# A four-layer graph network with norms on one core: the order of the second graph layer's DVE work, its output bias, and the addition ahead of the first norm

## The chip, the cores and the metric

One core of a Trainium2 chip runs the whole program. The metric is the device time of one execution in microseconds (us). Lower is better.

## The reference

There are 100,000 nodes with 16 features each, 50,000 edges sorted by destination, 16 features on each edge, and one of 8 types for each. Four layers follow one another, each added to its input and normed over the 16 features of a node:

```python
x = _layernorm(x + _L0_gnn_ref(x, edge_attr_16, ..., src, dst))   # per edge and feature a softmax over the edges of a node
x = _layernorm(x + _L1_gnn_ref(x, edge_index, W_tp, weight, bias))  # bilinear messages
x = _layernorm(x + _L2_gnn_ref(x, edge_index, eps1, w1a, ..., b2b)) # two graph layers, then log_softmax
x = _layernorm(x + _L3_gnn_ref(x, src, dst, edge_type_8, ...))      # typed messages, then a GRU cell

def _gin_conv(x, src, dst, eps, wa, ba, wb, bb, n_nodes):           # used twice in _L2
    agg = jax.ops.segment_sum(x[src], dst, num_segments=n_nodes)
    h = (1.0 + eps) * x + agg
    return jax.nn.relu(h @ wa + ba) @ wb + bb
def _layernorm(x, axis=-1, eps=1e-05):
    m = jnp.mean(x, axis=axis, keepdims=True)
    v = jnp.var(x, axis=axis, keepdims=True)
    return (x - m) / jnp.sqrt(v + eps)
```

The change touches the first norm, `x + _L0(x)`, and the second `_gin_conv` with its log_softmax and the third norm.

## The kernel before, in words

**Tiles.** Nodes are padded to 14 tiles (NODE_TILES) of 7168. A tile is 128 partitions x 896 columns (W): 56 nodes of 16 features on each partition, in 7 packs of 128 columns. Five engines run programs of their own (PE, DVE, ACT, POOL and SP, which issues the plain DMAs), each strictly in the order written; semaphores tie them together, and the order in the code is the schedule. The stages follow one another on the same node tables: the edge softmax; the first norm with the start of the sum by source; the bilinear layer; a sum by destination; `gin(0)`, the first graph layer; another sum by destination; `gin(1)`, the second graph layer; a third sum by destination; the GRU.

**First norm** (DVE from L1883, ACT from L972, PE from L1310, SP from L641). For each tile DVE adds the two loaded tiles `xin` and `ain` (L1884), sums over 16 features (L1751), centres into `xm` (L1753), sums the squares that ACT made (L1763; ACT's Square is L922), and scales with the factor that ACT made (L928 and L930) into the resident table `x1s` (L1770). From tile 3 on most tiles also carry one group of the expansion, which takes finished rows to slots of edges: ACT copies 8 blocks (L948), PE multiplies them with one-hot tiles (L1318), DVE makes the one-hot tile (L1783), masks the products (L1793) and reduces them (L1805), and POOL adds them into a table (L738). That is so for 10 of the 14 tiles; the other four (0 to 2 and 10) have the norm alone. PE's program holds only the expansion products there, and SP loads tile t+2 once tile t is scaled. After the last tile come further groups, and then POOL scatters 56 groups with 392 indirect DMAs (L755).

**Second graph layer**, `gin(1)`. In every tile DVE makes `yy` (L2033, `gin_ahead`), PE turns it (L1433), ACT copies that (L1089), PE multiplies with the first weights (L1444, L1445), ACT adds the bias and takes the Relu (L1098), and PE multiplies with the second weights, pack by pack, into `ps[2]` (L1456, `gin_out`). Then DVE adds the output bias into `zz` (L2040), takes the maximum over a node's 16 values (L2067) and subtracts it into `zcs` (L2072). ACT takes Exp (L1112), DVE sums (L2080), ACT takes Ln (L1120). POOL adds the layer's input to `zcs` (L794) and subtracts the logarithm (L797), in `gin_second`. Then the norm: DVE sums (L2088), centres into `xm` (L2091), ACT squares (L1127), DVE sums the squares (L2098), ACT makes the factor (L1134, L1136), and DVE scales (L2105). One round of DVE's loop (from L2109) reads:

```python
gin_ahead(1, t + 3)
gin_scale(t - 1)
gin_softmax(t + 1)      # L2040, L2067, L2072
if t < NODE_TILES:
    gin_centre(t)       # L2088, L2091
gin_sum(t + 1)
if t < NODE_TILES:
    gin_squares(t)
```

PE's round is `gin_out(t - 2)`, `gin_hidden(t - 1)`, `gin_turn(t)`; PE may write `ps[2]` again once L2040 has read it (semaphore `g_o`). SP (from L547) waits, tile by tile, for `yy` and then loads `xin`, for POOL's addition and then loads `ain`, for the scaling and then stores `yout`. After the last store POOL starts the gathers of the third sum by destination (L771).

## Time and profile before

| | |
|---|---|
| device time, 3 runs | 4698.01 us median, 4685.06 to 4700.72 |
| the profiled execution's own time | 4688.55 us |
| its span | 4686.7 us |
| granted TensorE clock, mean | 0.703 |
| DVE busy | 3340.9 us (71%) |
| POOL busy | 3240.6 us (69%) |
| PE busy | 2956.8 us (63%) |
| ACT busy | 1618.6 us (35%) |
| the chain that ended last | POOL 14%, issue 9%, DVE 5%, PE 3% |

Times are those of one execution, taken by the hardware profiler. Times of a timeline count from the start of the span. A line number is that of the instruction in the kernel; L440 and other helpers serve several callers. A group's mean covers the time of one instruction; the time from the start of one to the start of the next can be shorter, as consecutive ones overlap a little. The granted clock is the share of TensorE's full clock that the throttle passed in a stretch: 1.00 is 2.4 GHz and 0.50 is 1.2 GHz.

### The profile page before, as it was taken

To read this page: it belongs to the slowest core of one execution; us is meant where nothing else is said; L and a number is where in the kernel's file an instruction comes from. 1 tells how busy PE (TensorE), PEld (TensorE's weight loads), DVE (VectorE), ACT (ScalarE), POOL (GpSimd) and SP (SyncE) were. 2 spreads that over 40 slices of the span, in tenths; PEclk is the share of its full clock that TensorE was granted. 3 is DMA by queue.
4 is the path that set the end of the run, shared out by engine and by line. 5 is a ranking of instruction groups with operands and counts; after the bars stand their busy time and mean duration, and the time that the engine had idled before them with its cause. 6 is when DMAs were issued, how large, how long until landed. Compare 5 with 4: busy or idle time off the path is not lost. (4 is left out here: it accounts for less than half of the span.)

```text
span 4686.7 us, 58419 instructions
## 1 busy us (share of the span) xinstructions
PE 2956.8 (63%) x13925; PEld 2319.0 (49%) x13925; DVE 3340.9 (71%) x5631; ACT 1618.6 (35%) x4208; POOL 3240.6 (69%) x2831
## 2 busy tenths in 40 slices
PE   5888888888534444435999344473444546777686
PEld 2444444444334444434888234453344436777675
DVE  7999999999795555555888455663556784555678
ACT  3666666666441111102555111121111241222245
POOL 4777777777537888887999677726777337777422
PEclk8777778777665555557999566576556665555688
DMA  4222222222143333343322100031000240000022
GB/s 128 69 67 63 69 69 65 69 63 66 42 135 58 60 60 59 57 76 81 79 78 63 18 7 7 7 93 33 7 7 7 53 114 7 7 7 7 3 74 76
DMA packets 411137, 247.46 MB, mean 53 GB/s; under 512 B 107063, under 2 KB 370091, under 8 KB 410988
## 3 DMA queue, kind: packets, MB, share of 16 engines
q1 hardware_dynamic: 291708, 226.22, 17.4%
q0 software_dynamic: 119296, 19.68, 6.5%
q8 instruction: 58, 0.95, 0.1%
q14 instruction: 75, 0.61, 0.0%
HBM read 180.94 MB, written 64.76 MB: 52 GB/s over the span
## 5 line engine op out<-in xcount | busy, mean ns | idle before, releaser
L1375 PE MATMUL ps<-arena 128*128 128x128 f32 x2976 | 665.7, 413 | 619.3 <-DVE arena L1934 564.6
L771 POOL DMA_INDIRECT extra<-x_t,srci x784 | 767.1, 978 | 260.5 <-issue 245.3
L1375 PEld LDWEIGHTS ps<-arena 128*128 128x128 f32 x2976 | 618.3, 316 | 656.5 <-issue 647.6
L755 POOL DMA_INDIRECT sums<-cmb,sidx x392 | 613.1, 1564 | 136.3 <-issue 117.8
L1248 PE MATMUL ps<-arena,yout 128*128 128x512 f32 x784 | 565.3, 812 | 219.6 <-DVE arena L1725 210.3
L717 POOL DMA_INDIRECT xg<-in_x,xidx x392 | 443.8, 1132 | 203.6 <-issue 118.8
L704 POOL DMA_INDIRECT ft_t<-fts,fidx x392 | 469.2, 1197 | 146.6 <-issue 115.8
L1934 DVE TENSOR_TENSOR arena<-jmask,ps 128x1024 f32<-128x1024 f32 (+1 forms) x174 | 212.5, 1221 | 499.5 <-ACT ps L1030 491.4
L1951 DVE TENSOR_TENSOR arena<-arena,ps 128x128 f32 x1488 | 426.3, 286 | 182.0 <-DVE arena L1951 23.9
L771 POOL DMA_INDIRECT extra<-h_t,srci x392 | 369.9, 944 | 215.5 <-issue 210.9
L1318 PE MATMUL ps<-arena 128*128 128x128 f32 x992 | 224.6, 417 | 445.1 <-DVE arena L1783 347.0
L1030 ACT ACTIVATE ps<-extra 128x16 f32 x1392 | 160.2, 168 | 944.5 <-SPq L666 819.0
L1318 PEld LDWEIGHTS ps<-arena 128*128 128x128 f32 x992 | 208.1, 319 | 453.2 <-DVE arena L1783 352.7
L1417 PE MATMUL ps<-wb,arena 128*128 128x256 f32 x1568 | 355.3, 380 | 0.0
L1248 PEld LDWEIGHTS ps<-arena,yout 128*128 128x128 f32 x784 | 191.5, 259 | 311.7 <-DVE arena L1725 227.9
L1417 PEld LDWEIGHTS ps<-wb,arena 128*128 128x128 f32 x1568 | 291.2, 191 | 35.7
L440 POOL TENSOR_TENSOR extra<-arena 128x512 f32<-128x512 f32 x196 | 267.5, 1386 | 32.3 <-DVE arena L2005 16.1
L1681 DVE TENSOR_TENSOR_SCAN arena<-ps,arena,edge_in 128x512 f32<-128x512 f32 x196 | 240.5, 1268 | 10.3 <-PE ps L1250 10.3
L1699 DVE TENSOR_TENSOR_SCAN arena<-arena,ps 128x512 f32<-128x512 f32 x196 | 240.2, 1268 | 10.2
L1925 DVE TENSOR_TENSOR arena<-ps,relp 128x1024 f32<-128x1024 f32 x186 | 226.3, 1217 | 8.2 <-PE ps L1375 8.2
L1705 DVE TENSOR_TENSOR_SCAN arena<-arena 128x1026 f32<-128x1026 f32 x98 | 222.5, 2270 | 0.0
L960 ACT ACTIVATE cmb<-ps 128x112 f32<-128x112 f32 x56 | 14.7, 263 | 587.8 <-PE ps L1333 360.1
(257 smaller groups left out, 6407.5 us busy)
## 6 DMA issues: line engine op xcount, KB each, us to landing
edge_in<-in_ef SPq DMA_DIRECT2D x98, 256.0 KB
edge_in<-far_row SPq DMA_DIRECT2D x98, 256.0 KB
ain<-in_src_row SPq DMA_DIRECT2D x56, 448.0 KB, 3.7
sums<-zero SPq DMA_DIRECT2D x132, 144.0 KB
arena<-rel_t SPq DMA_DIRECT2D x63, 256.0 KB, 3.9
x_t<-yout SPq DMA_DIRECT2D x28, 448.0 KB, 3.4
xin<-x_t SPq DMA_DIRECT2D x28, 448.0 KB, 4.0
extra<-x_t,srci POOLq DMA_INDIRECT x784, 2.3
```

Source lines behind the costliest of these rows:

```text
L440: return eng.tensor_tensor(o.rearrange("p (s w u) -> p s w u", s=2, u=F), products.rearrange("p (s w u) -> p s w u", s=2, u=F), x_tile.rea ...
L704: pool.indirect_dma_start(ft_t, bass.IndirectOffsetOnAxis(ap=fidx[b][:, k:k + 1], axis=0), fts[b][:, k * F:(k + 1) * F], None).then_inc(ft ...
L717: pool.indirect_dma_start(xg[:, k, :], None, x, bass.IndirectOffsetOnAxis(ap=xidx[:, k:k + 1], axis=0)).then_inc(x_gathered, 16)
L755: pool.indirect_dma_start(sums[k], bass.IndirectOffsetOnAxis(ap=sidx[n % 2][:, j:j + 1], axis=0), cmb[n % 2][:, j, :], None, compute_op=AL ...
L771: pool.indirect_dma_start(dy[:, t, :], None, table, bass.IndirectOffsetOnAxis(ap=srci[:, t:t + 1], axis=0)).then_inc(d_gathered[n % QUEUE] ...
L1248: pe.matmul(o, wl[:, cols], outer[b][:, h * ET:(h + 1) * ET], start=True, stop=False)
L1318: last = pe.matmul(ps[b][:, j * P:(j + 1) * P], turned_oneh[b][:, j * P:(j + 1) * P], xblk[b][:, j * P:(j + 1) * P], start=True, stop=True)
L1375: last = pe.matmul(slot_sums(k, n)[:, j * P:(j + 1) * P], oneh[b][:, j * P:(j + 1) * P], placed[b][:, j * P:(j + 1) * P], start=True, stop ...
L1417: last = pe.matmul(bank_of(k)[:, 256 * s:256 * (s + 1)], sT[par_], wbk[j // 4][:, (j % 4) * 256:(j % 4 + 1) * 256], start=True, stop=True)
L1681: last = dve.tensor_tensor_scan(mx[b][:, h, 1:ET + 1], ps[0][:, h * ET:(h + 1) * ET], far[b][:, :], mx[b][:, h, 0:1], ALU.max, ALU.add)
L1699: last = dve.tensor_tensor_scan(by_half(num[o])[:, h, 1:ET + 1], by_half(dd[o])[:, h, 1:ET + 1], ps[1][:, h * ET:(h + 1) * ET], final(num[ ...
L1951: dve.tensor_tensor(o, o, slot_sums(k, c)[:, j * P:(j + 1) * P], ALU.add).then_inc(acc_done, 1)
```

## The change

In the first norm PE makes the sum of the two tiles, as two products with the identity that accumulate in `ps[3]`, for columns 0 to 511 and 512 to 895; DVE reads that sum from PSUM. DVE's round becomes: sum of tile t, scaling of tile t-1, centring of tile t, expansion, squares of tile t. ACT copies the blocks ahead of the square instead of behind it, PE puts each expansion group behind the tile's addition, and SP loads tile t+2 once PE has added tile t.

In the second graph layer PE adds the output bias: ahead of each of the 7 products of `gin_out` it multiplies a 3-row tile of ones with a 3-row tile that holds the bias as three 16-bit parts, into the same columns. L2040 is gone; the maximum and the subtraction read `ps[2]`, and PE waits for the subtraction (`l_zc`) before it writes there again. DVE's round becomes: subtraction of tile t, norm's sum of t-1, sum of exponentials of t, squares of t-2, maximum of t+1, scaling of t-2, centring of t-1, `yy` of t+4. ACT's round is put in a matching order. SP waits for POOL's addition before it loads `ain` two tiles on, and stores five tiles behind in place of two. `split_bias`, 10 small DVE instructions, runs once behind the sum by source. New tiles and the semaphore `bias_split` serve that.

```diff
@@ -255,2 +255,4 @@
         vvs = [vv[:, :], tile_of(13)]
+        out_bias, out_ones = sb("out_bias", [PARTS, P], BF16), sb("out_ones", [PARTS, P], BF16)
+        out_part, out_rest = sb("out_part", [PARTS, PARTS, F], BF16), sb("out_rest", [PARTS, 4, F])
         gate_set = [extra[:, 0:4 * UNIT], arena[:, (N_ACC + 1) * UNIT:(N_ACC + 5) * UNIT]]
@@ -546,3 +550,4 @@
                 sum_by_destination(ph - 2)
-                for t in range(NODE_TILES + 2):
+                ahead = 5 if ph in late_loads else 2
+                for t in range(NODE_TILES + ahead):
                     if t + 2 < NODE_TILES:
@@ -550,8 +555,8 @@
                         load(t + 2)
-                    n = t - 2
+                    if ph in late_loads and 2 <= t < NODE_TILES:
+                        wait(l_t, t - 1)
+                        load_late(t)
+                    n = t - ahead
                     if n < 0:
                         continue
-                    if ph in late_loads and n + 2 < NODE_TILES:
-                        wait(l_t, n + 1)
-                        load_late(n + 2)
                     wait(y_done, node_count(ph, 0, n) + 1)
@@ -646,3 +651,3 @@
                 for t in range(NODE_TILES):
-                    wait(y_done, t + 1)
+                    wait(v_done, t + 1)
                     load_nodes(t + 2)
@@ -962,6 +967,2 @@
 
-                def blocks_of(t, n, at):
-                    act.wait_ge(y_done, t)
-                    copy_blocks(0, n, at)
-
                 act.wait_ge(y_zero, 2)
@@ -969,9 +970,8 @@
                 for t in range(NODE_TILES):
-                    ready = first_tile_with(0, t)
-                    if ready:
-                        at = block_offsets(0, ready[0])
-                        norm(0, t // 2, t % 2, lambda t=t, n=ready[0], at=at: blocks_of(t, n, at))
-                        copied = ready[0] + 1
-                    else:
-                        norm(0, t // 2, t % 2)
+                    for n in first_tile_with(0, t):
+                        at = block_offsets(0, n)
+                        act.wait_ge(y_done, t)
+                        copy_blocks(0, n, at)
+                        copied = n + 1
+                    norm(0, t // 2, t % 2)
                 act.wait_ge(y_done, NODE_TILES)
@@ -1132,3 +1132,3 @@
                 n = node_count(2, 0, t)
-                act.wait_ge(s_own, 2 * n + 2)
+                act.wait_ge(s_own, 2 * n + (3 if t < NODE_TILES - 1 else 2))
                 act.activation(st[:, 2, :], st[:, 1, :], ACT.Ln, bias=eps_col[:, :], scale=1.0 / F).then_inc(s_ln, 1)
@@ -1137,9 +1137,10 @@
 
-            for t in range(-3, NODE_TILES):
+            for t in range(-2, NODE_TILES + 2):
+                gin_turned(1, t + 2)
+                gin_exp(t)
+                gin_ln(t)
+                gin_factor(t - 2)
                 gin_hidden(1, t + 2)
-                gin_turned(1, t + 3)
-                gin_exp(t + 1)
-                gin_square(t)
-                gin_ln(t + 1)
-                gin_factor(t)
+                if t <= NODE_TILES:
+                    gin_square(t - 1)
             sum_by_destination(2)
@@ -1321,3 +1322,15 @@
 
-                for n in range(AHEAD + 1):
+                expanded = 0
+                for t in range(NODE_TILES):
+                    wait_loaded(pe, 0, t // 2, t % 2)
+                    if t:
+                        pe.wait_ge(s_xm, t)
+                    for cols in (slice(0, 512), slice(512, W)):
+                        pe.matmul(ps[3][:, cols], ident, xin[t % 2][:, cols], start=True, stop=False)
+                        last = pe.matmul(ps[3][:, cols], ident, ain[t % 2][:, cols], start=False, stop=True)
+                    last.then_inc(v_done, 1)
+                    for n in first_tile_with(1, t):
+                        expand(n)
+                        expanded = n + 1
+                for n in range(expanded, AHEAD + 1):
                     expand(n)
@@ -1453,6 +1466,8 @@
                 if t:
-                    pe.wait_ge(g_o, n)
+                    pe.wait_ge(l_zc if q else g_o, t)
                 for g in range(PACKS):
-                    last = pe.matmul(ps[2][:, g * P:(g + 1) * P], hidden[:, g * P:(g + 1) * P], bd[2 * q + 1][:, :],
-                                     start=True, stop=True)
+                    o = ps[2][:, g * P:(g + 1) * P]
+                    if q:
+                        pe.matmul(o, out_ones[:, :], out_bias[:, :], start=True, stop=False)
+                    last = pe.matmul(o, hidden[:, g * P:(g + 1) * P], bd[2 * q + 1][:, :], start=not q, stop=True)
                 last.then_inc(g_ops, 1)
@@ -1467,2 +1482,3 @@
             sum_by_destination(1)
+            pe.wait_ge(bias_split, BIAS_MADE)
             gin(1)
@@ -1881,12 +1897,23 @@
                 expanded = 0
-                for t in range(NODE_TILES):
-                    wait_loaded(dve, 0, t // 2, t % 2)
-                    dve.tensor_tensor(vv[:, :], xin[t % 2][:, :], ain[t % 2][:, :], ALU.add).then_inc(v_done, 1)
-                    ready = first_tile_with(1, t)
-                    if ready:
-                        norm(0, 0, t // 2, t % 2, vv[:, :],
-                             [lambda n=ready[0]: expand_mask(0, n), lambda n=ready[0]: expand_sum(0, n)])
-                        expanded = ready[0] + 1
-                    else:
-                        norm(0, 0, t // 2, t % 2, vv[:, :])
+                v = slots(ps[3][:, 0:W])
+                for t in range(NODE_TILES + 1):
+                    if t < NODE_TILES:
+                        dve.wait_ge(v_done, t + 1)
+                        dve.tensor_reduce(st[:, 0, :], v, AX, ALU.add).then_inc(s_own, 1)
+                    if t:
+                        dve.wait_ge(s_sd, t)
+                        dve.tensor_tensor(slots(x1_of(0, t - 1)), slots(xm[:, :]), over(st[:, 3, :]),
+                                          ALU.mult).then_inc(y_done, 1)
+                    if t < NODE_TILES:
+                        dve.wait_ge(s_own, 2 * t + 1)
+                        if t:
+                            dve.wait_ge(y_done, t)
+                        dve.scalar_tensor_tensor(slots(xm[:, :]), over(st[:, 0, :]), -1.0 / F, v,
+                                                 ALU.mult, ALU.add).then_inc(s_xm, 1)
+                        for n in first_tile_with(1, t):
+                            expand_mask(0, n)
+                            expand_sum(0, n)
+                            expanded = n + 1
+                        dve.wait_ge(s_sq, t + 1)
+                        dve.tensor_reduce(st[:, 1, :], slots(sq_first), AX, ALU.add).then_inc(s_own, 1)
                 keys(0, 0)
@@ -1896,2 +1923,27 @@
 
+            def split_bias():
+
+                b = prm[0:PARTS, A_B2B:A_B2B + F]
+                part = lambda k: out_part[:, k, :]
+                rest = lambda k: out_rest[:, k, :]
+                at = lambda k: ident[0:PARTS, k:k + 1]
+                dve.memset(out_ones[:, :], 1.0).then_inc(bias_split, 1)
+                dve.tensor_copy(part(0), b).then_inc(bias_split, 1)
+                dve.wait_ge(bias_split, 2)
+                dve.tensor_tensor(rest(0), b, part(0), ALU.subtract).then_inc(bias_split, 1)
+                dve.wait_ge(bias_split, 3)
+                dve.tensor_copy(part(1), rest(0)).then_inc(bias_split, 1)
+                dve.wait_ge(bias_split, 4)
...
+                dve.wait_ge(bias_split, 9)
+                dve.tensor_copy(out_bias[:, :].rearrange("p (j f) -> p j f", f=F),
+                                rest(2).unsqueeze(1).broadcast_to((PARTS, PACK, F))).then_inc(bias_split, 1)
+
             def sum_by_destination(k):
@@ -1980,2 +2032,3 @@
             sum_by_source()
+            split_bias()
 
@@ -2059,3 +2112,5 @@
 
-            def gin_softmax(t):
+            FIRST_OWN = 2 * node_count(2, 0, 0)
+
+            def gin_maximum(t):
 
@@ -2065,4 +2120,8 @@
                     dve.wait_ge(l_zc, t)
-                gin_out(1, t)
-                dve.tensor_reduce(st[:, 6, :], slots(zz), AX, ALU.max).then_inc(l_max, 1)
+                dve.wait_ge(g_ops, NODE_TILES + t + 1)
+                dve.tensor_reduce(st[:, 6, :], slots(ps[2][:, 0:W]), AX, ALU.max).then_inc(l_max, 1)
+
+            def gin_shift(t):
+                if not 0 <= t < NODE_TILES:
+                    return
                 dve.wait_ge(l_max, t + 1)
@@ -2071,3 +2130,4 @@
                     dve.wait_ge(l_ex, t - 1)
-                dve.tensor_tensor(slots(zcs[t % 2]), slots(zz), over(st[:, 6, :]), ALU.subtract).then_inc(l_zc, 1)
+                dve.tensor_tensor(slots(zcs[t % 2]), slots(ps[2][:, 0:W]), over(st[:, 6, :]),
+                                  ALU.subtract).then_inc(l_zc, 1)
 
@@ -2081,12 +2141,16 @@
 
+            def gin_total(t):
+                if not 0 <= t < NODE_TILES:
+                    return
+                dve.wait_ge(v_done, node_count(2, 0, t) + 1 - NODE_TILES)
+                if t:
+                    dve.wait_ge(s_xm, node_count(2, 0, t))
+                dve.tensor_reduce(st[:, 0, :], slots(vvs[t % 2]), AX, ALU.add).then_inc(s_own, 1)
+
             def gin_centre(t):
-                if t < 0:
+                if not 0 <= t < NODE_TILES:
                     return
-                n = node_count(2, 0, t)
-                v = slots(vvs[t % 2])
-                dve.wait_ge(v_done, n + 1 - NODE_TILES)
-                dve.tensor_reduce(st[:, 0, :], v, AX, ALU.add).then_inc(s_own, 1)
-                dve.wait_ge(s_own, 2 * n + 1)
+                dve.wait_ge(s_own, FIRST_OWN + max(2 * t, 1))
                 dve.wait_ge(y_done, node_count(3, 0, t))
-                dve.scalar_tensor_tensor(slots(xm[:, :]), over(st[:, 0, :]), -1.0 / F, v,
+                dve.scalar_tensor_tensor(slots(xm[:, :]), over(st[:, 0, :]), -1.0 / F, slots(vvs[t % 2]),
                                          ALU.mult, ALU.add).then_inc(s_xm, 1)
@@ -2108,11 +2172,11 @@
             wait_sums(dve, 1)
-            for t in range(-3, NODE_TILES + 1):
-                gin_ahead(1, t + 3)
-                gin_scale(t - 1)
-                gin_softmax(t + 1)
-                if t < NODE_TILES:
-                    gin_centre(t)
-                gin_sum(t + 1)
-                if t < NODE_TILES:
-                    gin_squares(t)
+            for t in range(-4, NODE_TILES + 2):
+                gin_shift(t)
+                gin_total(t - 1)
+                gin_sum(t)
+                gin_squares(t - 2)
+                gin_maximum(t + 1)
+                gin_scale(t - 2)
+                gin_centre(t - 1)
+                gin_ahead(1, t + 4)
             sum_by_destination(2)
```

## Rows read from the trace of the kernel before

**Rows 1.** The page's line of busy time per engine over the span
```profile
PE 2956.8 (63%) x13925; PEld 2319.0 (49%) x13925; DVE 3340.9 (71%) x5631; ACT 1618.6 (35%) x4208; POOL 3240.6 (69%) x2831
```

**Rows 2.** Windows: stretch, its us, then busy us (instructions) per engine, PEclk, DMA
```profile
1282.00:1394.00 112.00, 39.01 (x170) 36.70 (x171) 103.06 (x103) 41.50 (x130) 37.10 (x74) 0.59 0.45 127
...
3700.00:3714.00 14.00, 7.62 (x43) 5.23 (x43) 12.86 (x11) 7.57 (x12) 8.09 (x4) 0.97 0.13 38
...
3714.00:3820.00 106.00, 64.36 (x234) 48.03 (x235) 104.85 (x85) 41.74 (x65) 34.17 (x18) 0.69 0.45 119
```

**Rows 3.** Timeline, DVE, one tile of the second layer: start us, us, instruction
```profile
3772.63 1.08 DVE L2040 TENSOR_TENSOR arena<-ps,prm 128x896 f32<-128x896 f32 x1
3773.74 1.09 DVE L2067 TENSOR_REDUCE st<-arena 128x56 f32<-128x896 f32 x1
3774.86 1.09 DVE L2072 TENSOR_TENSOR extra<-arena,st 128x896 f32<-128x896 f32 x1
3775.87 1.08 DVE L2088 TENSOR_REDUCE st<-vv 128x56 f32<-128x896 f32 x1
3776.98 2.08 DVE L2091 SCALAR_TENSOR_TENSOR xm<-st,vv 128x896 f32<-128x896 f32 x1
3778.99 1.07 DVE L2080 TENSOR_REDUCE st<-extra 128x56 f32<-128x896 f32 x1
3780.08 1.09 DVE L2098 TENSOR_REDUCE st<-arena 128x56 f32<-128x896 f32 x1
3781.09 2.06 DVE L2033 SCALAR_TENSOR_TENSOR arena<-xin,prm,arena 128x896 f32<-128x896 f32 x1
3783.07 1.08 DVE L2105 TENSOR_TENSOR yout<-xm,st 128x896 f32<-128x896 f32 x1
```

**Rows 4.** Timeline, POOL, the same tile: start us, us, instruction, idle before
```profile
3776.03 2.08 POOL L794 TENSOR_TENSOR extra<-extra,ain 128x896 f32<-128x896 f32 x1 [5.28 <-DVE extra L2072]
...
3780.49 1.71 POOL L797 TENSOR_TENSOR extra<-extra,st 128x896 f32<-128x896 f32 x1 [2.37 <-ACT st L1120]
```

**Rows 5.** One line of the bilinear stage: ns min/median/max of DVE from PSUM
```profile
L440 DVE TENSOR_TENSOR arena<-ps,arena x98: 675/691/693, 2174.0 to 2573.8; 128x512 f32<-128x512 f32 x98
```

**Rows 6.** Timeline, DVE: first subtraction and last scaling of the second layer
```profile
3699.80 1.09 DVE L2072 TENSOR_TENSOR extra<-arena,st 128x896 f32<-128x896 f32 x1
...
3854.68 1.09 DVE L2105 TENSOR_TENSOR yout<-xm,st 128x896 f32<-128x896 f32 x1 [0.69 <-ACT st L1136]
```

**Rows 7.** Timeline, PE: the layer's products at either clock
```profile
3690.88 2.07 PE L1444 MATMUL ps<-arena,bd 128*128 128x512 f32 x2 [1.01 <-ACT arena L1089]
...
3705.20 1.80 PE L1456 MATMUL ps<-bd,arena 128*128 128x128 f32 x14
...
3706.84 1.02 PE L1444 MATMUL ps<-extra,bd 128*128 128x512 f32 x2
...
3773.85 3.33 PE L1456 MATMUL ps<-bd,arena 128*128 128x128 f32 x14 [0.34 <-DVE arena L2040]
```

**Rows 8.** Groups by line and shape: 16-bit matmuls of 128 columns
```profile
L1292 PE MATMUL ps<-identb,xq 128*48 128x128 bf16 x784 | 40.5, 225 | 1.4 <-ACT ain L905 1.4
```

**Rows 9.** The page's DMA issues: KB each, us to landing
```profile
xin<-x_t SPq DMA_DIRECT2D x28, 448.0 KB, 4.0
```

**Rows 10.** Timeline, DVE, first norm: first addition, one tile, last scaling
```profile
1282.11 1.08 DVE L1884 TENSOR_TENSOR vv<-xin,ain 128x896 f32<-128x896 f32 x1
...
1312.26 1.10 DVE L1884 TENSOR_TENSOR vv<-xin,ain 128x896 f32<-128x896 f32 x1
...
1320.44 1.11 DVE L1884 TENSOR_TENSOR vv<-xin,ain 128x896 f32<-128x896 f32 x1
...
1392.58 1.08 DVE L1770 TENSOR_TENSOR arena<-xm,st 128x896 f32<-128x896 f32 x1
```

**Rows 11.** Timeline, PE, first norm: one group of expansion products
```profile
1318.63 3.76 PE L1318 MATMUL ps<-arena 128*128 128x128 f32 x16 [4.64 <-issue]
```

**Rows 12.** Timeline, DVE: the wait behind the sum by source
```profile
2174.04 0.69 DVE L440 TENSOR_TENSOR arena<-ps,arena 128x512 f32<-128x512 f32 x1 [30.61 <-PE ps L1417]
```

10 lines of the change are left out of this document (added).

## The prediction

> **What bounds the kernel now.** First the page's busy shares [rows 1]: no engine is busy beyond 71%, so the kernel is a chain of stages, each with a bound of its own, and the two stages of the change have to be read by themselves. Then the windows [rows 2]: in the first norm DVE is busy for 103.06 of 112 us, in the body of the second graph layer for 104.85 of 106 us. DVE sets the pace in both, while PE has room (39 and 64 us busy) and runs at a mean granted clock of 0.59 and 0.69. Both stages stand between stages that need their whole result, so what they lose in time the kernel loses.
>
> Then DVE's timeline of one tile of the layer [rows 3]. Nine instructions make a round. The steps from start to start are 1.00 us, or 1.11 where an instruction needs the result just made, except that L2091 and L2033 take 2.08 and 2.06 us. Beside them [rows 4]: POOL's L794 runs from 3776.03 to 3778.11, and L2091, started at 3776.98, ends at 3779.06; POOL's L797 runs from 3780.49 to 3782.20, and L2033 ends at 3783.15. Both end 0.95 us behind POOL, as if begun then: a DVE instruction with two operands in SBUF stands still while POOL works. The sums L2088, L2080 and L2098 overlap POOL and take 1.07 to 1.09. The nine steps add up to 11.44 us a tile (to 3784.07, a step of 1.00 behind the last row), 2 us of it blocked.
>
> **Layer, DVE's part.** L2040 goes: 1.0 us a tile. The new order puts two sums, the sum of squares and the maximum behind the subtraction, the time in which POOL works, and scaling, centring and yy behind those. Does the subtraction or the maximum cost more for reading PSUM? L2040 reads PSUM in 1.08 us, L2072 reads SBUF in 1.09 [rows 3], and 98 DVE instructions that take one operand from PSUM and one from SBUF beside a POOL stage take 675 to 693 ns, none blocked [rows 5]. I take 1.09 for both. The Trainium skill (VectorE: DVE Perf Modes, section Rules for kernel authors) advises copying a matmul's result to SBUF where several operations follow; by it dropping L2040 gains nothing, and the sum would be 14 us smaller. The trace shows no such price for one read; two reads in a row no run here shows.
>
> The round, from the subtraction's start at 0: norm's sum at 1.0; sum of exponentials at 2.2 (it needs ACT's Exp over 896 columns, an estimate of one DVE instruction's length behind the subtraction); squares at 3.2; maximum at 4.2; scaling at 5.2. POOL's second instruction starts 1.5 us behind the start of L2080 [rows 3, 4], so at 3.7, and ends at 5.4; the scaling then ends at 6.35. Centring starts at 6.45, yy at 7.45, the next subtraction at 8.6. **8.6 us** a tile is what DVE allows.
>
> **Layer, PE's part, and the new wait.** The maximum of tile t+1 waits for PE's product, and that for the subtraction of tile t, since both use ps[2]. Behind the waiting maximum on DVE stand scaling, centring, yy and the next subtraction, and POOL waits for that. The chain is 1.15 (subtraction and signal) + product + 4.2 (maximum, scaling, centring, yy, signals) us. The product took 1.80 us at the high clock and 3.33 at the low one [rows 7]. The bias adds seven 16-bit products of 3 rows by 128 columns with a weight load each. The trace has none such. Below: 0.05 us each, as L1292 at 40.5 us for 784 [rows 8]. Above: each costs as much as the 32-bit product beside it, 1.8 us a tile more at the high clock, 3.3 at the low. I take 0.07 and 0.14 each, near L1292, to which they are nearest in type and width: 2.3 us at the high clock, 4.3 at the low. The chain gives 7.65 us (DVE's 8.6 stands) or **9.65 us**.
>
> Which clock? Before, PE stood idle for 41.6 of 106 us, 4.5 in each round, and began the burst of 3773.85 at the low clock; from 3700 to 3714 the granted clock was 0.97 [rows 2, 7]. After, the round is shorter and PE's work longer: high-clock work is 2.3 + 1.7 (L1444 of 1.02 and L1445 of three quarters of that, less overlap) + 1.0 (turning, half of L1456) = 5.0 of 8.6 us, so idle time shrinks to 3.6 us but doesn't go; at the low clock it is about 9.5 of 9.65. The two states feed on each other, and I expect a mixture: **9.2 us**.
>
> The sum: the first subtraction moves from 3699.80 [rows 6] to about 3701.0, since yy of tile 3 and the bias come before it. Two first rounds without norm work (6.2, 7.2), eight full ones (73.6), three without yy (24.6), then 7.5, 5.1 and 3.9 for the tail: 128.1 us, to 3829 in place of 3855.8 (3854.68 + 1.09, rows 6). **26 us** gained; at 8.6 a round 34, at 9.65 19.
>
> What hides the rest: SP moves the same 42 transfers. A load of xin is issued behind POOL's addition of two rounds before its use, some 12 us ahead, and lands in 4.0 [rows 9]; without that cover a round would grow by up to 4 us. The stores are five tiles behind, but the last follows the last scaling directly. ACT has under 5 us of work a round. `split_bias` is 10 instructions of at most 0.3 us each, 3 us, inside DVE's 30.61 us wait for the scatters of the sum by source [rows 12]; without that cover it would cost 3 us.
>
> **First norm.** From 1282.11 to 1393.66 [rows 10] is 111.5 us: 10 tiles with expansion at 8.18 (1312.26 to 1320.44), 81.8 us, and four others with 29.7, 7.4 each. The addition L1884 goes: 1.0 us a tile, so DVE allows 7.2. In its place PE multiplies twice 512 and 384 columns: twice 1.7 us at the high clock, 3.4 in all; 6.7 at the low, from L1444 at 1.02 and 2.07 [rows 7]. It starts when the centring has freed ps[3], and behind it come DVE's sum, scaling and centring: 3.3 us. So the chain is 3.3 + 3.4 = 6.7 us or 3.3 + 6.7 = 10.0. PE also has the expansion, 3.76 us at the low clock [rows 11], about 2.0 at the high: together 5.4 or 10.5 us a tile. DVE's one-hot, mask, reduction and squares fill the time of PE's addition. At the high clock: 72 + 4 x 6.7, + 3.0 for the cold first product and the last scaling, 102: 9 us gained. I take an addition of 4.1 us on average, so 7.4 with expansion and 7.8 on the others, which start cold: 74 + 31 + 3 = 108. **3 us** gained. SP's loads come earlier than before, ACT's copies hide behind the addition on PE. POOL's scatters start when the expansion is ahead enough, and so move with the norm's end.
>
> Sum: 26 + 3 = 29 us off the profiled execution's 4688.55, 4659.5. The median of the runs, 4698.01, lies 9.5 above that execution: **4669 us**.
>
> **The rivals.**
> A. *The clock stays high in both stages.* For it: 0.97 between 3700 and 3714 at 54% busy [rows 2]. Against it: the idle time of 3.6 us. 34 + 9 = 43 us: 4655.
> B. *The low clock in the layer.* Each burst begins behind a wait, as L1456 of 3.33 us does now [rows 7]; then the maximum waits for PE in each round: 9.65 us, 19 gained, and the norm's additions average over 5 us and lose 5: 14 us, 4684. The Trainium skill (TensorE: Matmul & The Clock Gate, section HAM oscillation) says that bursts parted by waits on data start over at half clock; by that rule this case is the forecast. The trace of before agrees for bursts 4.5 us apart.
> C. *Slower: the addition on PE.* With the low clock throughout the norm PE needs 10.5 us a tile with expansion and 10.0 on the others: 105 + 40 + 3 = 148, 36 us lost, against 19 gained in the layer: 4715. It loses in the norm from an addition of 4.9 us (3.3 + 4.9 = 8.2) and outweighs the layer from about 6. If the bias also has its upper price, PE needs 6.7 + 3.6 + 1.7 = 12.0 us a round, over 11.44, and about 10 more are lost: 4744. Against it: PE would be 100% busy, and dense stretches had the high clock.
> D. *The change doesn't free DVE of POOL*: POOL's instructions reach the scaling or the centring and block them for another 1 us a round. 14 us of the gain go: 4683. For it: POOL's second instruction ends at 5.4 us, within the scaling's turn.
>
> **The numbers.** Chances: forecast 0.48, A 0.25, B 0.16, C 0.06, D 0.05. About 0.3% (14 us) is what a measurement of this kernel can tell from no change. Forecast, A and half of D are faster, B is at the edge and mostly no change, C slower: 0.77, 0.17, 0.06. The range runs from 4648 (A, and 7 us for the spread of the runs, which is 16 us before) to 4692 (B with a norm that loses 10 more); C and the ends of A are left out.
>
> **What would show it.** L2040 and L1884 are gone; L2091, L2033 and L2105 take 1.1 us each, and only the scaling may show 1.2 where POOL ends late. The round is near 9.2 us, with a short wait of the maximum for L1456's line where PE is at the low clock; the granted clock of the layer is over 0.8, that of the norm too. The norm ends 3 us earlier, the layer is 26 us shorter, and the stages between keep their length. Waits of DVE for PE of over 1.5 us a round would mean B or C; L2105 of 2 us would mean D; scatters or gathers that take longer would make the sum wrong altogether.

## The result: 0.4% slower

| | before | after |
|---|---|---|
| median of 10 runs each, us | 4694.84 (4685.06 to 4701.16) | 4714.89 (4706.31 to 4722.66) |
| ratio of the runs, 95% interval | 1 | 1.004 (1.0031 to 1.0048) |
| profiled execution and its span, us | 4688.55, 4686.7 | 4710.06, 4708.3 |
| first norm, DVE's first one-hot tile to the end of the last scaling, us | 112.2 | 113.1 |
| second layer, first yy to last scaling's end, us | 168.9 (3686.91 to 3855.77) | 189.8 (3686.64 to 3876.39) |
| a full round of that layer, us | 11.44 | 12.5 to 13.0 |

4669 us was forecast, with a range to 4692. The span grew by 21.6 us, 20.9 of them in the second layer. The norm took 0.9 us longer, but it began 1.2 us earlier, and the stages between kept their length, so the layer began as early as before (3686.64 for 3686.91). The last 0.9 us lie behind the layer.

### The profile after

The page's busy line, then the windows (PE, PEld, DVE, ACT and POOL busy, granted clock, DMA share, GB/s) of the norm and of the layer's body; they answer to [rows 1, 2]:

```profile
PE 3026.8 (64%) x14041; PEld 2341.9 (50%) x14135; DVE 3291.6 (70%) x5613; ACT 1618.4 (34%) x4208; POOL 3222.0 (68%) x2831
```

```profile
1282.00:1394.00 112.00, 74.84 (x281) 44.91 (x280) 89.10 (x90) 42.02 (x130) 22.61 (x78) 0.88 0.47 133
3714.00:3820.00 106.00, 85.13 (x264) 52.26 (x265) 69.08 (x67) 36.44 (x57) 32.47 (x17) 0.63 0.33 96
```

In the layer's body DVE is busy for 69 us where it was for 105, and PE for 85 where it was for 64: DVE no longer sets the round, and PE, which doesn't fill it either, runs at a clock of 0.63, lower than before (0.69). DVE's timeline of one tile, which answers to [rows 3]:

```profile
3765.40 1.09 DVE L2131 TENSOR_TENSOR extra<-ps,st 128x896 f32<-128x896 f32 x1
3766.41 1.08 DVE L2148 TENSOR_REDUCE st<-vv 128x56 f32<-128x896 f32 x1
3767.51 1.09 DVE L2140 TENSOR_REDUCE st<-extra 128x56 f32<-128x896 f32 x1
3768.51 1.08 DVE L2162 TENSOR_REDUCE st<-arena 128x56 f32<-128x896 f32 x1
3773.37 1.09 DVE L2122 TENSOR_REDUCE st<-ps 128x56 f32<-128x896 f32 x1 [3.78 <-PE ps L1472]
3774.38 1.08 DVE L2169 TENSOR_TENSOR yout<-xm,st 128x896 f32<-128x896 f32 x1
3775.57 1.09 DVE L2155 SCALAR_TENSOR_TENSOR xm<-st,vv 128x896 f32<-128x896 f32 x1
3777.42 1.15 DVE L2086 SCALAR_TENSOR_TENSOR arena<-xin,prm,arena 128x896 f32<-128x896 f32 x1 [0.76 <-PE ps L1446]
3778.49 1.08 DVE L2131 TENSOR_TENSOR extra<-ps,st 128x896 f32<-128x896 f32 x1
```

DVE does what was forecast of it: eight instructions, each 1.07 to 1.15 us, none blocked by POOL, no price for reading PSUM. But twice a round it waits for PE: the maximum 3.78 us for the product, yy 0.76 us for the turning. PE's timeline of the next product, and its weight loads:

```profile
3779.72 0.21 PE L1471 MATMUL ps<-out_bias,out_ones 3*128 3x128 bf16 x1 [2.40 <-DVE extra L2131]
...
3780.35 0.28 PE L1471 MATMUL ps<-out_bias,out_ones 3*128 3x128 bf16 x1
3780.57 0.80 PE L1472 MATMUL ps<-bd,extra 128*128 128x128 f32 x2
3781.29 0.28 PE L1471 MATMUL ps<-out_bias,out_ones 3*128 3x128 bf16 x1
...
3785.85 1.92 PE L1457 MATMUL ps<-arena,bd 128*128 128x512 f32 x2
3787.56 1.49 PE L1458 MATMUL ps<-arena,bd 128*128 128x384 f32 x2
3788.84 1.49 PE L1446 MATMUL ps<-cst,arena 128*128 128x128 f32 x6
```

```profile
3780.35 0.10 PEld L1471 LDWEIGHTS ps<-out_bias,out_ones 3*128 3x128 bf16 x1 [0.19 <-issue]
3780.57 0.50 PEld L1472 LDWEIGHTS ps<-bd,extra 128*128 128x128 f32 x2
3781.29 0.10 PEld L1471 LDWEIGHTS ps<-out_bias,out_ones 3*128 3x128 bf16 x1 [0.22 <-issue]
```

A pack (bias product and 32-bit product) takes 3781.29 - 3780.35 = 0.94 us at the low clock from start to start. The loads tell why: each begins together with its own product (3780.57 in both fences), so none is hidden behind the product ahead of it. The product's phase, from its first start to its last end, is 5.7 to 6.6 us in the layer's body; all at the low clock it is 6.63, where it was 3.33 [rows 7]. So a bias product adds (6.63 - 3.33)/7 = 0.47 us, where 0.14 was forecast. Over the layer the wait for the product sums to:

```profile
L2122 DVE TENSOR_REDUCE st<-ps 128x56 f32<-128x896 f32 x14 | 15.3, 1092 | 45.6 <-PE ps L1472 45.6
```

The wait of yy for the turning adds 18.6 us. In the norm a tile takes 7.23 us of DVE as forecast, in four rounds 8.3 or 8.4, and in the first ones 7.3, 9.5 and 8.2, where PE's addition runs at the low clock. Two rows 7.23 apart:

```profile
1330.18 1.08 DVE L1902 TENSOR_REDUCE st<-ps 128x56 f32<-128x896 f32 x1
1337.41 1.08 DVE L1902 TENSOR_REDUCE st<-ps 128x56 f32<-128x896 f32 x1
```

### The profile page after: what moved, and what is told of

Read it like the earlier page. It is cut to its first block and busy times, and to the rows that moved or that the text cites. A ratio compares the mean times of both kernels' runs of the same rounds, so it can differ in the third digit from the quotient of the medians.

```text
span 4708.3 us, 58767 instructions
## 1 busy us (share of the span) xinstructions
PE 3026.8 (64%) x14041; PEld 2341.9 (50%) x14135; DVE 3291.6 (70%) x5613; ACT 1618.4 (34%) x4208; POOL 3222.0 (68%) x2831
## 5 line engine op out<-in xcount | busy, mean ns | idle before, releaser
L1388 PE MATMUL ps<-arena 128*128 128x128 f32 x2976 | 656.2, 409 | 626.5 <-DVE arena L1986 569.8
L1388 PEld LDWEIGHTS ps<-arena 128*128 128x128 f32 x2976 | 608.6, 311 | 663.8 <-issue 652.3
L1319 PE MATMUL ps<-arena 128*128 128x128 f32 x992 | 207.7, 394 | 351.7 <-DVE arena L1799 351.7
L1319 PEld LDWEIGHTS ps<-arena 128*128 128x128 f32 x992 | 194.1, 299 | 360.3 <-DVE arena L1799 357.2
L1715 DVE TENSOR_TENSOR_SCAN arena<-arena,ps 128x512 f32<-128x512 f32 x196 | 240.2, 1268 | 10.2
```

What stands on the lines that cost most here:

```text
L1319: last = pe.matmul(ps[b][:, j * P:(j + 1) * P], turned_oneh[b][:, j * P:(j + 1) * P], xblk[b][:, j * P:(j + 1) * P], start=True, stop=True)
L1388: last = pe.matmul(slot_sums(k, n)[:, j * P:(j + 1) * P], oneh[b][:, j * P:(j + 1) * P], placed[b][:, j * P:(j + 1) * P], start=True, stop ...
L1715: last = dve.tensor_tensor_scan(by_half(num[o])[:, h, 1:ET + 1], by_half(dd[o])[:, h, 1:ET + 1], ps[1][:, h * ET:(h + 1) * ET], final(num[ ...
```

## The experiments

Eighteen kernels, in five batches; each kernel is compared with runs of the kernel before on the same chip. For e1 to e5, e7, e11, e12, e19 and e20 the kernel before took 5290 to 5331 us; the rest of the program is longer there, but the old second layer takes 168.7 us (e2), as here. So compare ratios and stages across batches, not times. "Layer" is first yy to last scaling's end; windows are the same 106 us of its body, 27 us behind the first yy.

### One part alone

**e1_layer_only, e2_norm_only**: the change with the old norm; the old layer with the new norm (nothing of the rest differs).

> The changed kernel's second layer lasts 189.8 us in its profile (3686.6 to 3876.4), 168.9 before; its first norm 113.1 us, 112.2 before. Theory P (the seven narrow bias products on PE make the layer slower, all else is even): with the layer's part of the change alone and the old norm, the layer lasts 188 to 191 us and the time is 19 to 22 us over the kernel before, ratio 1.004. Rival N (the norm's addition on PE loses the time, for instance in what follows it): ratio 1.000 to 1.001.

> The norm's part of the change alone. Theory P: the norm is even, first one-hot to last scaling 111 to 114 us, the layer is the old one of 168.9 us, ratio 1.000. Rival N: 15 us or more over before, ratio 1.003 or more.

Measured: layer only 1.0057 (1.0037 to 1.0078), rounds 12.6 to 13.0, layer 188.0 us. Norm only 0.999 (0.9969 to 1.0011), layer 168.7. The loss is the layer's. The norm's ratio can't be told from 1, but its profile differs from that of the changed kernel. From the first one-hot tile to the last scaling e2 takes 106.0 us:

```profile
1364.88 0.75 DVE L1790 TENSOR_SCALAR arena<-arena,sl_s 128x1024 f32<-128x1024 bf16 x1 [25.66 <-DMA arena<-rel_t]
...
1469.82 1.09 DVE L1896 TENSOR_TENSOR arena<-xm,st 128x896 f32<-128x896 f32 x1 [0.69 <-ACT st L930]
```

The old norm takes 112.1 to 112.2 in each of its six profiles. The new norm takes 106.0 to 106.2 in those of e2, e3, e4 and e7 and 111.2 to 113.2 in the ten others. The code is the same; what differs is the clock at which the additions of the first tiles run (0.94 over e2's first 30 us, 0.75 over those of the changed kernel).

**e3_no_bias**: the seven bias products are left out, and so the output lacks the second layer's output bias.

```diff
-                    o = ps[2][:, g * P:(g + 1) * P]
-                    if q:
-                        pe.matmul(o, out_ones[:, :], out_bias[:, :], start=True, stop=False)
-                    last = pe.matmul(o, hidden[:, g * P:(g + 1) * P], bd[2 * q + 1][:, :], start=not q, stop=True)
+                    last = pe.matmul(ps[2][:, g * P:(g + 1) * P], hidden[:, g * P:(g + 1) * P], bd[2 * q + 1][:, :],
+                                     start=True, stop=True)
```

> The changed kernel with the seven bias products left out; the output bias is not added, nothing else differs. Theory P: each costs PE about 0.46 us at the low clock (a step of 0.94 from pack to pack against 0.47 before), 3.3 us a tile. The round goes from 12.9 us to 9.3 to 10.3, the layer lasts 145 to 157 us, and the time is 10 to 22 us below before, ratio 0.995 to 0.998. Rival O (the new order itself is too long: turning, yy, subtraction and product in one ring): the round stays at 11.4 us or more, the layer at 169 or more, ratio 1.000 or more.

```profile
4166.00:4272.00 106.00, 54.50 (x259) 41.78 (x257) 100.26 (x96) 52.59 (x84) 45.87 (x25) 0.80 0.46 134
```

Measured: 0.9951 (0.9929 to 0.9973), rounds 8.4 to 9.0, layer 138.1 us. The whole loss, and a gain of 31 us in the layer that it hides, hang on the bias products. With them gone the clock is 0.80, although PE is busy for 54 us in place of 85.

**e7_dve_bias**: the new order, but DVE adds the bias again (nine instructions), PE has no bias.

```diff
-                dve.wait_ge(g_ops, NODE_TILES + t + 1)
-                dve.tensor_reduce(st[:, 6, :], slots(ps[2][:, 0:W]), AX, ALU.max).then_inc(l_max, 1)
+                gin_out(1, t)
+                dve.tensor_reduce(st[:, 6, :], slots(zz), AX, ALU.max).then_inc(l_max, 1)
...
```

> The changed kernel's new order and norm, but the bias is again added by DVE (PSUM to SBUF, with the old line's add), and PE multiplies no bias; maximum and subtraction read SBUF; ps[2] is free once DVE's addition has read it. Theory: DVE has nine steps of 1.0 to 1.15 us and none blocked by POOL, so 9.3 to 9.6 us a round; PE's product of 3.3 us starts behind DVE's addition, which is early enough, so waits for PE stay under 0.7 us a round. Layer 148 to 156 us in place of 168.9 before and 189.8 after, ratio 0.996 to 0.9975. This says that the new order alone is worth 13 to 20 us and the move of the bias costs more than it brings. Rival (the new order itself brings the waits for PE, not the bias): rounds over 11 us, ratio at or over 0.999.

Measured: 0.9979 (0.9953 to 1.0004), full rounds of 9.5 us, layer 145.6. The order alone is worth 23 us of the stage, more than the 13 to 20 expected; the ratio's interval is wide and just reaches 1.

### Why a bias product costs 0.47 us

**e4_bias_wide, e5_bias_seven_first**: the bias ahead of the seven 32-bit products, as two wide products or as the same seven narrow ones in a row.

```diff
+                    pe.matmul(ps[2][:, 0:512], out_ones[:, :], out_bias[:, 0:512], start=True, stop=False)
+                    pe.matmul(ps[2][:, 512:W], out_ones[:, :], out_bias[:, 0:W - 512], start=True, stop=False)
...
```

> The changed kernel with the bias added by two wide products (512 and 384 columns) ahead of the seven 32-bit ones, so with one load of the ones. Theory P, form S (the price is the alternation of 16-bit and 32-bit products, which keeps the next weights from being loaded ahead): the two cost 0.8 us at the low clock, the round is 9.6 to 10.8 us, the layer 148 to 160 us, ratio 0.996 to 0.999. Form C (the price goes by columns of bias): 896 columns as before, no gain over the changed kernel, round 12 or more, ratio 1.003 or more.

> The changed kernel, but with the seven narrow 16-bit bias products of a tile in a row, ahead of the seven 32-bit products (same bytes, same instructions, other order). Theory P (the price is the alternation: in the changed kernel the load of a 32-bit product behind a bias product is not drawn ahead, 0.94 us a pack in place of 0.47 at the low clock): in a row the bias products take about 0.1 us each, the 32-bit ones 0.47 again, the product's phase 4.0 to 4.3 us in place of 6.1 to 6.6; layer's rounds of 10.0 to 10.4 us as with the two wide products, ratio to the kernel before 0.998. Rival Q (the price is the number of products and loads, each narrow one costs some 0.4 us wherever it stands): phase over 6 us, rounds 12.5 to 13, ratio 1.004.

```profile
4168.89 0.90 PE L1470 MATMUL ps<-out_bias,out_ones 3*128 3x128 bf16 x7 [2.40 <-DVE extra L2133]
```

Measured: e4 0.9978 (0.996 to 0.9995), rounds of 10.1 to 10.2 behind two of 9.4 and 8.4, layer 148.2; e5 0.9989 (0.9962 to 1.0016), rounds of 10.0 to 10.2, layer 151.0. The same seven products that add 3.3 us between the others take 0.90 in a row, 0.13 each. The price is that of going to and fro, not of number or size (rival Q falls). But between what and what: types, or shapes?

**e6_bias_32bit**: bias and ones in FP32, alternating.

```diff
-        out_bias, out_ones = sb("out_bias", [PARTS, P], BF16), sb("out_ones", [PARTS, P], BF16)
+        out_bias, out_ones = sb("out_bias", [PARTS, P]), sb("out_ones", [PARTS, P])
```

> The changed kernel with the bias and its ones in FP32 in place of BF16, alternating as there. It tells whether the price comes from the change of type between neighbours or from the additional product and load as such. If from the change of type: without it the loads are drawn ahead, a bias product costs little more than its own columns, and a pack takes well under 0.94 us at the low clock, rounds of 10 to 12 us. If from the additional product beside a 32-bit one (each 32-bit product costs 0.47 us at the low clock whatever its rows): 0.94 us a pack, rounds of 12.5 to 13, ratio 1.003 to 1.005, the upper bound of the prediction (a bias product costs as much as the 32-bit product beside it).

```profile
3764.63 0.79 PE L1471 MATMUL ps<-out_bias,out_ones 3*128 3x128 f32 x2
3765.35 0.80 PE L1472 MATMUL ps<-bd,arena 128*128 128x128 f32 x2
3766.07 0.79 PE L1471 MATMUL ps<-out_bias,out_ones 3*128 3x128 f32 x2
```

Measured: 1.0158 (1.0143 to 1.0174), rounds of 16.0 to 16.4, a pack 1.44 us. Both expectations were too low: with one type throughout, a bias product costs 0.72 us beside a 32-bit product that also takes 0.72, not 0.48. So it isn't the type; what still alternates is the number of rows, 3 and 128.

**e8_rows_128, e15_rows_64, e16_rows_96**: the changed kernel with bias and ones on more rows, zero beyond the third; all else the same.

```diff
-        out_bias, out_ones = sb("out_bias", [PARTS, P], BF16), sb("out_ones", [PARTS, P], BF16)
+        out_bias, out_ones = sb("out_bias", [P, P], BF16), sb("out_ones", [P, P], BF16)
...
+                dve.memset(out_bias[:, :], 0.0).then_inc(bias_split, 1)
```

> The changed kernel with bias and ones on 128 rows in place of 3 (rows 3 to 127 zero), all else the same. Theory: the price is the load and the step, not the rows, and the clock doesn't depend on the rows that a product uses: 0.94 us a pack at the low clock, granted clock near 0.63 to 0.65 in the layer's body, rounds of 12.5 to 13, ratio 1.003 to 1.005. Rival (products of three rows count for little with the clock gate, so that PE looks idle in 40% of its busy time and stays low): granted clock over 0.8 and rounds under 11 us.

> As the kernel with bias and ones on 128 rows, but on 64 (rows 3 to 63 zero). Theory T (the load of the 128-row product is drawn ahead only beside a product that uses all rows; behind one with fewer it starts when that has been issued): 64 rows are fewer than 128, so a pack takes 0.57 us at the high and 0.94 at the low clock as with 3 rows, and rounds are 12 to 13 us, ratio 1.003 to 1.005. Rival U (the price falls with the rows step by step, since it is the clock that counts active rows): the pack's step at each clock as with 128 rows (0.33 and 0.64 us), rounds between 9 and 12.

> The same with 96 rows. Theory T in its strict form: fewer than 128, so as with 3 rows, 0.57 and 0.94 us a pack, rounds of 12 to 13. T in its loose form (what matters is whether the product takes the array in full height or as a part of it, and 96 rows no longer fit a half): 0.33 and 0.64 us a pack, rounds of 8.4 to 9.6, ratio 0.995, as with 128 rows. Rival U: between the runs with 64 and 128 rows.

PE's timeline with 128 rows at the high and the low clock and its loads, then with 64 rows at both clocks, then with 96 at the high one:

```profile
3778.00 0.22 PE L1471 MATMUL ps<-out_bias,out_ones 128*128 128x128 bf16 x1
3778.05 0.44 PE L1472 MATMUL ps<-bd,extra 128*128 128x128 f32 x2
3778.33 0.22 PE L1471 MATMUL ps<-out_bias,out_ones 128*128 128x128 bf16 x1
```

```profile
3770.04 0.74 PE L1472 MATMUL ps<-bd,arena 128*128 128x128 f32 x2
...
3770.68 0.74 PE L1472 MATMUL ps<-bd,arena 128*128 128x128 f32 x2
```

```profile
3778.00 0.30 PEld L1472 LDWEIGHTS ps<-bd,extra 128*128 128x128 f32 x2
3778.22 0.10 PEld L1471 LDWEIGHTS ps<-out_bias,out_ones 128*128 128x128 bf16 x1
```

```profile
3769.04 0.21 PE L1471 MATMUL ps<-out_bias,out_ones 64*128 64x128 bf16 x1 [2.41 <-DVE extra L2132]
...
3769.61 0.23 PE L1471 MATMUL ps<-out_bias,out_ones 64*128 64x128 bf16 x1
...
3770.45 0.28 PE L1471 MATMUL ps<-out_bias,out_ones 64*128 64x128 bf16 x1
...
3771.39 0.28 PE L1471 MATMUL ps<-out_bias,out_ones 64*128 64x128 bf16 x1
```

```profile
3769.10 0.22 PE L1471 MATMUL ps<-out_bias,out_ones 96*128 96x128 bf16 x1
3769.16 0.44 PE L1472 MATMUL ps<-bd,arena 128*128 128x128 f32 x2
3769.43 0.22 PE L1471 MATMUL ps<-out_bias,out_ones 96*128 96x128 bf16 x1
```

| rows of the bias product | pack, start to start, high / low clock, us | whole product of seven packs, high / low, us | clock in the body | rounds, us | layer, us | ratio (interval) |
|---|---|---|---|---|---|---|
| no bias (before) | | 1.80 / 3.33 | 0.69 | 11.44 | 168.9 | 1 |
| 3 (after; high clock from e11) | 0.57 / 0.94 | 4.10 / 6.63 | 0.63 | 12.5 to 13.0 | 189.8 | 1.004 (1.0031 to 1.0048) |
| 64 | 0.57 / 0.94 | 4.18 / 6.62 | 0.64 | 12.4 to 13.0 | 187.1 | 1.0033 (1.0019 to 1.0046) |
| 96 | 0.33 / 0.64 | 2.50 / 4.64 | 0.77 | 8.4 to 10.4 | 153.5 | 0.9954 (0.9938 to 0.9969) |
| 128 | 0.33 / 0.64 | 2.49 / 4.64 | 0.84 | 8.4 to 9.6 | 144.1 | 0.9951 (0.9935 to 0.9966) |

This settles what the price hangs on, against my own expectation for 128 rows. It jumps between 64 and 96 rows and doesn't change from 3 to 64, which is T in its loose form. A bias product costs (4.10 - 1.80)/7 = 0.33 us at the high and 0.47 at the low clock on 3 rows, 0.10 and 0.19 on 128. With 96 or more rows the load of the next product starts 0.11 us before that product and under the one ahead (load 3778.22, product 3778.33); with 64 or fewer it starts with its own product, and the two switches of a pack cost 0.24 us (0.57 - 0.33) at the high clock and 0.30 at the low. In the Trainium skill, the page TensorEngine Tiling (Array Packing), section Key Properties, says that changing the tiling mode drains TensorE. The section Available Configurations there lists heights of 32, 64 and 128 rows. These runs agree with both if a plain product on few rows counts as such a mode, which the page doesn't say: 3 and 64 rows fit a lower height, 96 don't. By that reading, which no run tests otherwise, the changed kernel switches fourteen times a tile.

The price is not all that the rows change. In e16 the rounds of the body whose product is wholly at the low clock (4.64 us) last 10.3 to 10.4. So of the way from 12.8 us to e8's mean of 8.9, some 2.4 are the price and the rest is the clock.

### The granted clock

**e17_wide_rows_128; e19_wide_3_old_norm, e20_wide_128_old_norm**: two wide bias products as in e4, on 128 rows; then the same pair, 3 and 128 rows, with the old norm and side by side on one chip. Here PE goes from 128 rows to 3 and back once a tile, in place of seven times, so little of the time is the price itself: the product takes 2.29 us with 3 rows and 2.10 with 128, both at the high clock.

> Two wide bias products a tile (512 and 384 columns) as in the kernel with 3 rows and one bank (rounds 10.1 us, granted clock 0.73, phase 0.85 + 3.35 us at the low clock), but on 128 rows. Here the load of a 128-row product stands behind a bias product only once a tile, so what is left is the clock. Theory V (products on few rows keep the granted clock low): clock over 0.8, the seven products in 1.9 us in most rounds, rounds of 8.4 to 9.0, ratio 0.994 to 0.996. Rival (the clock follows the waits and the busy time alone): rounds stay at 10.0 to 10.2 and the clock at 0.73, ratio 0.998.

> Two wide bias products a tile on 3 rows, one bank, norm of the kernel before; beside its twin on 128 rows, on the same chip. Both theories: as with the new norm, rounds of 10.0 to 10.2 us, granted clock 0.73 in the layer's body, layer 147 to 149 us, ratio 0.997 to 0.998.

> Its twin with bias and ones on 128 rows, no other difference. Theory V (products on few rows, and the 32-bit products behind them, are what keeps the granted clock low; seen so far only between two chips): clock 0.83 to 0.86, rounds of 8.4 to 9.4, layer 138 to 141 us, ratio 0.993 to 0.995. Rival (the chips differ, not the rows): the same rounds and clock as its twin within 0.2 us and 0.02.

The windows of e19 and of e20:

```profile
4168.00:4274.00 106.00, 78.53 (x291) 52.13 (x290) 89.59 (x86) 47.94 (x76) 42.72 (x24) 0.71 0.43 126
```

```profile
4174.00:4280.00 106.00, 56.35 (x284) 43.59 (x287) 99.02 (x95) 52.66 (x82) 46.93 (x25) 0.85 0.46 134
```

Measured: e17 0.994 (0.9927 to 0.9954), clock 0.85, rounds 8.4 to 9.4, layer 139.0. e19 0.9983 (0.9958 to 1.0008), clock 0.71, rounds 10.2, layer 153.8; e20 0.9968 (0.9946 to 0.9991), clock 0.85, rounds 8.4 to 9.8, layer 141.1. The layer of e19 is longer than expected and the ratio of e20 smaller a gain than expected, and the two ratios can't be told apart; the stages and clocks can. Some 0.8 us of three-row products a round goes with a clock of 0.71 in place of 0.85, although PE is then busier (78.5 us for 56.4, in part because its work takes longer at the low clock). So with one bank the rows move the clock. How was not told apart, whether through the products themselves, through the pause of the switch, or through the waits that a longer product brings; and the next experiments show that the rows alone don't decide it.

### The ring

The ring is the chain that closes on itself through `ps[2]`: PE's product waits for the subtraction of the tile before, the maximum waits for the product, and the next subtraction stands behind the maximum. A bank here is one such buffer of 896 columns in PSUM.

**e11_two_banks**: the product goes to ps[2] and ps[3] by turns, all seven alternating three-row bias products kept. **e12_wide_two_banks, e13_two_banks_old_norm, e18_all**: with the wide bias; with the old norm; with 128 rows too.

```diff
-                if t:
-                    pe.wait_ge(l_zc if q else g_o, t)
+                if q and t > 1:
+                    pe.wait_ge(l_zc, t - 1)
+                elif t and not q:
+                    pe.wait_ge(g_o, t)
+                bank = ps[3] if q and t % 2 else ps[2]
...
```

> The changed kernel with all seven alternating bias products, but the product goes to ps[2] and ps[3] by turns, so that it waits for the subtraction of two tiles before and no more for the last one. Theory R (the loss is the ring: product behind subtraction, maximum behind product, yy behind turning; PE itself has room, 85 of 106 us busy): with the ring open a round is DVE's 8.4 us or PE's own work, whichever is more. PE's work without gaps is about 10.7 us a round at the clock seen (85 us in 8.3 rounds are 10.3): rounds of 10.3 to 11.9 us if the low clock stays; if PE without gaps is granted the high clock, its work is about 7 us and the round 8.4 to 8.8, ratio 0.995. Rival (it is PE's work alone, at the low clock 11.9 to 12.5 us a round whatever the banks): rounds stay at 12 to 13, ratio 1.003 to 1.004.

> Two wide bias products a tile in place of seven narrow ones, and the product to ps[2] and ps[3] by turns; norm as in the changed kernel. Theory: PE's work is 0.85 + 3.35 + 3.2 + 1.2, about 8.6 us a round at the low clock, and doesn't wait for the last subtraction: rounds of 8.3 to 8.8 us, DVE's limit, layer 138 to 142 us, ratio about 0.995 (as without any bias). Rival (yy behind turning keeps the rounds at 9.5 to 10.1 as with one bank): ratio 0.998.

> Two wide bias products and two banks, with the norm as in the kernel before (DVE makes the addition). Theory: the norm's change is worth nothing either way (it lost 1.0 us in the trace of after), so this is as the same kernel with PE's addition: layer 137 us, rounds 8.45, ratio 0.992 to 0.995, to be held against 0.9936. Rival: PE's busy norm heats into a lower clock or later stages, and the old norm gains a further 3 us or more there: ratio under 0.992.

> Everything that helped together: two wide bias products on 128 rows, ps[2] and ps[3] by turns, the norm of the kernel before. Theory: DVE sets the round (8.45 us) with 3 rows and two banks already, so 128 rows change nothing in the rounds: layer 134 to 135 us as with 3 rows, ratio 0.9925 to 0.9935. Rival (the last tiles and the first, which PE's clock sets, shorten too): 131 us, ratio 0.992.

```profile
4175.00:4281.00 106.00, 85.86 (x351) 53.89 (x350) 100.88 (x96) 52.59 (x83) 48.40 (x26) 0.77 0.46 134
```

Measured: e11 0.9975 (0.9951 to 0.9999), rounds of 8.4 to 8.5, layer 141.1. The window is e11's: PE is busy for nearly the same time as in the changed kernel (86 for 85 us of 106), and yet DVE sets the round. The expensive bias costs the full rounds nothing once PE's product isn't locked between two DVE instructions; the first and last rounds keep some of it (141.1 us for e12's 137.0). And with the same busy time and the same seven three-row products PE is granted 0.77 here and 0.63 there. e12 0.9936 (0.9914 to 0.9958), layer 137.0; e13 0.9931 (0.9917 to 0.9944), 134.9; e18 **0.9926 (0.9913 to 0.994)**, 135.2 us, the lowest ratio, though its interval overlaps those of e12, e13 and e17. All of them beat both kernels. The norm's change makes no difference here that the ratios could show (e12, e13). With the wide bias and two banks the rows hardly matter to the clock either, 0.82 with 3 (e13) and 0.84 with 128 (e18):

```profile
3720.00:3826.00 106.00, 56.54 (x274) 39.24 (x273) 101.14 (x98) 52.27 (x84) 45.62 (x24) 0.82 0.47 137
3716.00:3822.00 106.00, 53.63 (x270) 40.04 (x268) 101.14 (x98) 52.28 (x84) 45.64 (x24) 0.84 0.47 137
```

**e14_turn_second**: one bank and alternating bias, PE's turning ahead of the hidden product.

```diff
                     gin_out(q, t - 2)
+                    if q:
+                        gin_turn(q, t)
                     gin_hidden(q, t - 1)
-                    gin_turn(q, t)
+                    if not q:
+                        gin_turn(q, t)
```

> The changed kernel with one bank and alternating bias products, but in the second layer PE turns yy of tile t between the product of t-2 and the hidden layer's product of t-1, in place of behind both. Theory: the wait of yy for the turning (0.2 to 2.25 us a round, 18.6 us in all) goes, since the turning ends some 3 us earlier; what stays is subtraction 1.2, product 6.5, maximum, scaling, centring, yy 4.4: rounds of 11.9 to 12.2 us in place of 12.5 to 13.0, layer 178 to 184 us, ratio 1.002 to 1.003. Rival (the wait only moves: the product then stands behind a later hidden product and ACT's copy, and the maximum waits longer): rounds stay 12.5 to 13.

Measured: 1.0021 (1.0012 to 1.003), rounds of 10.7 to 12.2, layer 179.9. The order of PE's work is worth 10 us of the 21: in full rounds yy no longer waits for the turning. The rounds fall below the 11.9 expected in part, since PE's clock is a little higher (0.65).

## Why the prediction was wrong

**Right.** L2091 and L2033 stood still for POOL, and in the new order nothing does (1.07 to 1.15 us each). At rounds of 8.45 us too the scaling takes only 1.18 (e13, median), so rival D falls. Maximum and subtraction read PSUM in 1.08 to 1.09 us, and dropping the copy gained its full 1.0 us (rounds of 9.48 in e7, 8.45 in e11). The Trainium skill (VectorE: DVE Perf Modes, section Rules for kernel authors) advises the copy where many operations follow; for these two reads the runs show no gain from it. `split_bias` took 2.2 us inside DVE's wait, which fell from 30.61 to 27.81 us. DVE's limit in the layer was put at 8.6 us a round; e11 to e13 show 8.45.

**Wrong, first and most: the price of the bias product**, "I take 0.07 and 0.14 each, near L1292, to which they are nearest in type and width". Measured: 0.33 and 0.47 us. At the low clock that is the upper bound (3.3 us a tile), and at the high one 2.3 us a tile, over the bound of 1.8. With one bank the product stands in the ring, so every round paid it. The nearest row was chosen by type and width. What decides is the number of rows: L1292 uses all 128 [rows 8], the bias 3. On 128 rows the same product costs 0.10 and 0.19 us, near the values taken, and the layer takes 144.1 us where the sum came to 143 (168.9 less 26). That closeness is in part luck: its eight full rounds last 8.9 us on average for the 9.2 taken, and the rounds ahead of and behind them make up for it.

**Wrong: the clock**, "the granted clock of the layer is over 0.8". It was 0.63, and is 0.84 with 128 rows. The step that more work in less idle time gives a higher clock failed: PE was busy for 85 us in place of 64 and got less. (The burst of before that the prediction dates from 3773.85 begins with the turning at 3771.76, 3.44 us behind the work ahead of it; its idle time lies in such gaps of 3.4 to 4.6 us.) Rival B had the low clock. The rule named there, that of the Trainium skill (TensorE: Matmul & The Clock Gate, section HAM oscillation) on bursts parted by waits, was nearer than the forecast. But waits alone don't tell the clock: e20 idles for longer than e19 (50 of 106 us for 27) and has the higher one, and e11 idles as long as the changed kernel (20 for 21) and has 0.77 for 0.63. What sets the clock stays open.

**Missed: yy behind the turning.** The chain was 1.15, the product and 4.2, and ended at yy. But yy has one buffer, so it also waits for the turning of the last tile, and that stands on PE behind product and hidden product: 0.2 to 2.25 us a round. With the product's 6.5 us the chain gives 11.9, the rest to 12.8 is this wait. With the turning put first (e14) the wait is gone and the rounds are 10.7 to 12.2.

**The norm**: a gain of 3 us was forecast. Its profile here shows a loss of 0.9, those of four experiments a gain of 6, so 3 lies between and isn't confirmed. Six rounds take 7.23 to 7.25 us, but the first ones 7.3, 9.5 and 8.2 and four later ones 8.3 or 8.4, where the reduction waits 1 to 4 us for an addition that runs at least in part at the low clock. In e2 the second and third round take 6.7. The ratio of e2 can't show 6 us in 5300.

**Rival C** put the slower case in the norm and gave the layer's half, a bias at its upper price and so 12.0 us of work on PE a round, as an addition to it. The upper price is what happened, and by itself enough. But PE's work didn't fill the round as C had it (85 of 106 us busy): the ring did, since with the same products and two banks the round is 8.45 us (e11).

## What to carry to other kernels

Before a small matmul is put between full ones, compare the rows it uses: a product on 64 rows or fewer between products on 128 cost 0.33 us at the high and 0.47 at the low clock here, on 96 or 128 rows (zeros in the rest) 0.10 and 0.19. Where it can't be widened, issue all of them in a row (seven took 0.90 us). And when DVE's work becomes shorter by reading PSUM directly, ask what the bank's later release does: one bank between product and subtraction put the product's whole time on the path, a second bank took it off.

## What was unexpected of the hardware

- Using fewer rows saves nothing: 3 and 64 rows cost the same, 96 and 128 cost the same, and the step between is 0.24 us a pack at the high and 0.30 us at the low clock.
- A three-row product in FP32 beside 128-row ones makes both take 0.72 us (e6), where seven 128-row ones in a run take 3.33, so 0.48 each.
- With one bank, some 0.8 us a round of three-row products went with a granted clock of 0.71 for 0.85 over the whole stretch, at more busy time (e19, e20); with two banks it was 0.82 for 0.84 (e13, e18).
- The same first norm took 106 us in some executions and 111 to 113 in others, by the clock that the additions of its first tiles were granted.
